# Mix and experts in one block, full units first, keys split step by step, half of the residual loaded early

## What is computed

```python
# x: [8, 1024, 256]
x = x + attn_ref(layernorm(x), ...)       # time mix (a scan over the tokens) and channel mix
x = x + ffn_ref(layernorm(x), ...)        # mixture of experts

def ffn_ref(x, expert_sel, keys, values): # 32 experts, 4 per token
    xt = x.reshape(-1, 256)
    gates = sigmoid(xt @ expert_sel.T)                      # [8192, 32]
    sel_val, sel_idx = top_k(gates, 4)
    gate_full = zeros.at[rows, sel_idx].set(sel_val)
    scores = relu(einsum('nd,edf->nef', xt, keys)) * gate_full   # keys   [32, 256, 128]
    return einsum('nef,efv->nv', scores, values)                 # values [32, 128, 256]
```

## Time and profile before

| | |
|---|---|
| runs | 1553.26, 1555.19, 1561.76 us; median 1555.19 |
| profiled execution | 1552.88 us, of which the span from first to last instruction is 1551.0 |
| PE busy | 1230.0 us (79%) |
| DVE busy | 1021.2 us (66%) |
| ACT busy | 782.7 us (50%) |
| POOL busy | 822.8 us (53%) |
| DMA traffic | 192.81 MB, mean 124 GB/s |

### The profile page before, as it was taken

How to read it: one execution, slowest core, us unless ns; L and a number is a source line. 1 busy time by engine, 2 the same in 40 slices (tenths; PEclk the granted TensorE clock), 3 DMA queues, 4 the chain that set the end, 5 groups by cost and what they waited for, 6 DMA issues and landing times. The chain is left out here.

```text
span 1551.0 us, 30666 instructions
## 1 busy us (share of the span) xinstructions
PE 1230.0 (79%) x8007; PEld 1118.6 (72%) x8008; DVE 1021.2 (66%) x2346; ACT 782.7 (50%) x1489; POOL 822.8 (53%) x902
## 2 busy tenths in 40 slices
PE   6799999999999999999974098988888888984000
PEld 5688888888888888888864087888888878883000
DVE  4788897878987788877746444444444444441799
ACT  3666676566764567555646045554555555542000
POOL 1524676666765676665656535555555555554000
PEclk9799999999999999999986579888889898787555
DMA  6000221212211121211163644444444444445998
GB/s 193 14 28 8 76 76 62 76 42 75 75 61 61 48 82 65 68 68 46 70 236 116 183 134 146 136 140 147 137 142 145 141 142 136 147 142 157 398 412 341
DMA packets 119841, 192.81 MB, mean 124 GB/s; under 512 B 17379, under 2 KB 93421, under 8 KB 118385
## 3 DMA queue, kind: packets, MB, share of 16 engines
q1 hardware_dynamic: 82672, 114.03, 23.2%
q0 software_dynamic: 26112, 67.68, 12.2%
q10 hardware_dynamic: 11008, 10.52, 2.0%
HBM read 101.09 MB, written 95.26 MB: 127 GB/s over the span
## 5 line engine op out<-in xcount | busy, mean ns | idle before, releaser
L1451 POOL DMA_INDIRECT expert_rows<-y,dest x288 | 285.7, 992 | 257.7 <-issue 216.1
L1180 POOL DMA_INDIRECT lists<-rows,slot x256 | 294.9, 1152 | 74.7 <-issue 71.3
L1356 PE MATMUL ps<-xt_hi,keys 128*128 128x128 f32 x1152 | 261.5, 311 | 56.0 <-ACT keys L1400 41.6
L1356 PEld LDWEIGHTS ps<-xt_hi,keys 128*128 128x128 f32 x1152 | 220.1, 224 | 67.3 <-issue 63.6
L1427 DVE TENSOR_TENSOR xt_lo<-ps,xt_hi 128x512 fp32r<-128x512 f32 x144 | 99.5, 691 | 218.7 <-ACT xt_hi L1384 183.0
L1396 ACT ACTIVATE y<-ps 128x512 f32<-128x512 f32 x144 | 86.8, 603 | 183.1 <-PE ps L1372 118.5
L1356 PE MATMUL ps<-xt_lo,keys 128*128 128x128 f32 x576 | 176.6, 307 | 2.0 <-issue 2.0
L582 PE MATMUL ps<-wv_hi,k_hi 128*128 128x256 f32 x512 | 151.5, 296 | 6.7 <-issue 6.5
L584 PE MATMUL ps<-wv_lo,k_hi 128*128 128x256 f32 x512 | 148.9, 291 | 4.0 <-issue 4.0
L586 PE MATMUL ps<-wv_hi,k_lo 128*128 128x256 f32 x512 | 148.5, 290 | 2.8 <-issue 2.8
L1342 PE MATMUL ps<-consts,xr 128*128 128x128 f32 x576 | 104.6, 313 | 35.7 <-DMA xr<-lists 34.1
(11 more groups left out here) (202 smaller groups left out, 3509.8 us busy)
## 6 DMA issues: line engine op xcount, KB each, us to landing
xr<-lists SPq DMA_DIRECT2D x288, 130.0 KB
ye<-expert_rows SPq DMA_DIRECT2D x32, 1024.0 KB, 20.9
x_sb<-in_x SPq DMA_DIRECT2D x16, 512.0 KB, 3.9
residual<-xp SPq DMA_DIRECT2D x16, 512.0 KB
experts_raw<-in_expert_in SPq DMA_DIRECT2D x8, 1024.0 KB, 24.4
resid<-residual SPq DMA_DIRECT2D x4, 2048.0 KB, 16.2
out_dram<-resid ACTq DMA_DIRECT2D x32, 256.0 KB, 8.3
expert_rows<-y,dest POOLq DMA_INDIRECT x288
```

Source lines behind the costliest of these rows:

```text
L1180: pool.indirect_dma_start(lists, bass.IndirectOffsetOnAxis(ap=slot[:, q, n:n + 1], axis=0), rows[:, q, n // TOPK, :], None).then_inc(held_ ...
L1356: mm = pe.matmul(ps[:, H + q % HBANKS, c], keys[:, q, s, half, k * DE:(k + 1) * DE], m[:, q, k, c], start=n == 0, stop=n == 3 * KD - 1)
L1451: pool.indirect_dma_start(expert_rows, bass.IndirectOffsetOnAxis(ap=dest[:, r, s:s + 1], axis=0), y[:, r, s, :], None, bounds_check=OUT_RO ...
```

## The change

- The blocks of the mix and of the experts become one: both functions return a routine for each engine, and an engine goes from its mix routine to its expert routine without a barrier. What the barrier ordered is ordered by waits: SyncE waits for the plan and for all scatters but the last tile's; the compute engines for the plan and for the split weights. Two tiles that the last scatters read (`rows_odd`, `slot`) get places of their own.
- The plan has two parts for each expert. First come the units that are full before the last tile's rows are counted (whole units of the count then), for all 32 experts; then the rest. The tables for this have 64 rows instead of 32. SyncE's steps up to EARLY (104 of 144) read full units only; behind that it waits for the last scatters, the fills and the cleared area.
- The keys are no longer split beforehand: `experts_raw` keeps them. Only the values are split, all eight pieces ahead of the last tile's routing. In each step ScalarE rounds the keys of both units (two instructions of 128x256), and VectorE makes their lo parts one step later (two subtractions of 128x256), the first thing in its step. TensorE waits for these.
- The residual's first two pieces are loaded by SyncE before the fills, as soon as the last tile's channel mix is done with the memory they take; the other two after the last product.
- The wait of SyncE for the last store of `residual` moves ahead of the fills; SyncE and ScalarE no longer wait behind their fills.

```diff
+EARLY = ((N - TILE) * TOPK - E * (UNIT - 1)) // UNIT // (SUB * RING) * RING
-ROUND_FIRST, SPLIT_FIRST = 3, 4
-HELD = 8
+ROUND_FIRST = 6
+RESID_AHEAD = 2
@@ program
         with ExitStack() as mix:
-            mix_phase(nc, mix, sem, locals())
+            mixing = mix_phase(nc, mix, sem, locals())
...
+            running = expert_phase(nc, experts, sem, locals())
+            with nc.Block() as block:
+                @block.sync
+                def _(sp):
+                    mixing[0](sp)
+                    running[0](sp)
...
@@ mix_phase, SyncE
             run(sp, step)
-            fill(sp, 0, E // 2)
             for stored in x1_stored:
                 sp.wait_ge(stored, 16 * NT // 2)
+        sp.wait_ge(val_ready, NT)
+        for n in range(RESID_AHEAD):
+            load_resid(sp, resid, residual, resid_loaded[0], n)
+        fill(sp, 0, E // 2)
@@ fill
-        eng.wait_ge(filled, 16 * E)
@@ round_experts, ScalarE
-                act.activation(experts_w[:, 0, part(n), :], experts_raw[:, part(n), :],
+                act.activation(values_hi[:, part(n), :], experts_raw[:, part(n), KD * DE:],
                                ACT.Copy).then_inc(experts_rounded, 1)
@@ mix_phase, VectorE
-                    split_experts(0, SPLIT_FIRST)
+                split_experts(0, LOADS)
...
             make_plan()
-            dve.wait_ge(scattered[1], 16 * (NT // 2 * J * TOPK - HELD))
-            split_experts(SPLIT_FIRST, LOADS)
@@ overflow_homes
+            chained_over(dve.tensor_copy(blocks_i[:], count[:]))
+            chained_over(dve.tensor_scalar(blocks_i[:], blocks_i[:], UNIT.bit_length() - 1, None,
+                                           ALU.logical_shift_right))
+            chained_over(dve.tensor_copy(early[:], blocks_i[:]))
+            dve.tensor_copy(units[:, 0:E], early[:])
+            dve.tensor_copy(offset[:, 0:E], early[:])
+            dve.tensor_copy(full_late[:, 0:E], zeros[:, 0:E])
+            chained_over(dve.tensor_copy(full_late[:, E:PARTS], full[:]))
@@ mix_phase, GpSimd
             run(pool, step)
-            pool.wait_ge(scattered[0], 16 * NT // 2 * J * TOPK)
-            pool.wait_ge(scattered[1], 16 * (NT // 2 * J * TOPK - HELD))
-            pool.wait_ge(held_scattered, 16 * HELD)
@@ expert_phase, SyncE
-            loop(sp, step)
+        sp.wait_ge(plan_ready, 1)
+        sp.wait_ge(scattered[0], 16 * NT // 2 * J * TOPK)
+        sp.wait_ge(scattered[1], 16 * (NT // 2 - 1) * J * TOPK)
+        for i in range(RING):
+            step(i, i, 0)
+        with sp.Fori(1, EARLY // RING) as ring:
+            for r in range(RING):
+                step(RING * ring + r, r, ring)
+
+        sp.wait_ge(last_scattered, 16 * J * TOPK)
+        sp.wait_ge(filled, 16 * E)
+        sp.wait_ge(area_cleared, 16 * (LIST_ROWS - OVERFLOW) // UNIT)
+        with sp.Fori(EARLY // RING, NSTEPS // RING) as ring:
+            for r in range(RING):
+                step(RING * ring + r, r, ring)
         sp.wait_ge(y_done, NSTEPS)
-            for n in range(RESID_PIECES):
+        for n in range(RESID_AHEAD, RESID_PIECES):
+            load_resid(sp, resid, residual, resid_loaded[1], n)
@@ expert_phase, ScalarE
-                    act.activation(keys[:, q, 1], w[:, :, bass.ds(e, 1), 0:KD * DE].rearrange(
-                        "p h a w -> p (h a) w"), ACT.Copy).then_inc(keys1_ready, 1)
+                for s, e in enumerate(experts):
+                    ins = act.activation(keys[:, q, s, 0, :], raw_keys(e), ACT.Copy)
+                ins.then_inc(keyhi_ready, 1)
@@ expert_phase, VectorE
+            if lagging(i, K_LAG):
+                b, q = i - K_LAG, (r - K_LAG) % SLOTS
+                if r == 0:
+                    expert[b % RING if isinstance(b, int) else RING - 1] = of_units(dve, plan_expert, b, E - 1)
+                dve.wait_ge(keyhi_ready, b + 1)
+                for s, e in enumerate(expert[(r - K_LAG) % RING]):
+                    ins = dve.tensor_tensor(keys[:, q, s, 1, :], raw_keys(e), keys[:, q, s, 0, :].bitcast(F32),
+                                            ALU.subtract)
+                ins.then_inc(keylo_ready, 1)
             if enters(i):
-                    dve.tensor_copy(keys[:, q, 0], w[:, :, bass.ds(expert[r], 1), 0:KD * DE].rearrange(
-                        "p h a w -> p (h a) w").bitcast(F32)).then_inc(keys0_ready, 1)
```

1840 lines of the change are left out of this document (931 added, 909 removed).

## The result

The changed kernel took 1580.91, 1577.33, 1573.04 and 1585.0 us, median 1579.12, beside 1554.54 for the kernel before on the same chip. The ratio of the runs is 1.0143, 95% interval 1.0104 to 1.0182 (the two medians alone would give 1.0158). Forecast were 1544, range 1532 to 1560. The profiled execution of after has a span of 1579.1 us, that of before 1551.0.

What follows compares the result with a forecast made beforehand. GpSimd's burst of four scatters was taken to pace the expert loop. 1552.9 − 7.5 (middle) − 8.5 (end) + 6 (loop) = 1542.9, raised to 1544 because the profiled execution lay under the median; range 1532 to 1560.

Steps and rivals of the forecast that it cites:

- that the mix stands still: Mix, ahead of everything the change touches: the prediction gave it no term.
- I take GpSimd's burst as the pace-setter.: Expert loop: GpSimd's four scatters per two-step period set its length; each 0.1 us a period is 7.2 us in all.
- The 0.08 us a period, +6 in all: Expert loop: VectorE's subtractions lengthen GpSimd's issues by 0.08 us a period, +6 us; bounds 0 and +18.
- slower: TensorE's slack ends: Expert loop rival: VectorE's holds reach the next y, 20 us each, giving 1558; decides from 16 us; chance 0.17.
- over 2: Expert loop, sign of the held case: TensorE waits for lo keys or `xt_lo` over 2 us a period.
- The second half, 8.9 us, lay beside the fills and is gone: nothing by itself.: Middle, beside the fills: dropping VectorE's second half of the split, 8.9 us, changes the time by nothing.
- Barrier and wait: Middle: without the barrier and the wait for fills the first load comes earlier, gain 6.9 to 8.4, taken as -7.5 us.
- The end: After the last product: less residual to load and possibly a shorter DRAIN, gain 6.2 to 10.7, taken as -8.5 us.
- Loads ahead, ScalarE, the plan.: Two residual loads before the fills, ScalarE's extra instruction a step, seven plan instructions: each taken as 0.

Runs made afterwards that it cites:

- the pause: One small GpSimd instruction and a wait for it, some 0.5 us, ahead of the 15th scatter of each tile; in the kernel before 1554.7 us against 1579.4.
- l1: Changed kernel with each of a step's two subtractions replaced by a one-operand reduction (lo part left wrong): 1593.5 us, ratio 1.0100 to the kernel before.
- b1: Kernel before, unedited, run again on a chip without stops beside the changed kernel: 1378.9 us.
- a1: Changed kernel, unedited, run again on a chip without stops: 1367.6 us, ratio 0.9915 to the kernel before.
- m2: Changed kernel with the pause, first set: 1561.3 us, ratio 0.9889 to the kernel before.
- m4: Changed kernel with the pause, the same kernel as m2 on another chip: 1563.6 us, ratio 0.9896 to the kernel before.
- m1: Kernel before with `rows_odd` and `slot` placed outside the mix's own tiles, no instruction added or moved: 1584.7 us, ratio 1.0064 to the unedited one.
- m3: Kernel before with the pause: 1554.7 us, ratio 0.9850 to the unedited one.
- f1: Changed kernel with GpSimd waiting for the 32 fills before the last tile's 16 scatters: 1597.4 us, ratio 1.0103 to the kernel before.

## Why the prediction was wrong

- **The step that failed most: that the mix stands still.** The prediction has no term for it, since no instruction of it moves. It took 23.0 of the 28.1 us. The kernel before holds the same 20 us as a lottery of its own (1554 on one chip, 1560 to 1581 and 1568 to 1590 on the next two, 1555 there with the pause). Its three runs, 8.5 us apart, were a sign, and so were the two tiles of 52.9 and 57.1 us in its trace, a weaker one, as they are longer than the rest without stops too. I read neither. My range took in only the terms that I had added up.
- **"I take GpSimd's burst as the pace-setter."** Wrong as it stands. Taking the lengthening away from GpSimd (l1) didn't shorten the loop, and without stops TensorE sets the pace. The 0.08 us a period, +6 in all, was the right effect but too small (mean issue 992 to 1043 ns is 14.7 us in all, 0.20 a period, within the 0 to 18), and on an engine that doesn't count: where stops are, the loop grew by 14.2 to 18.2 us, and where they aren't, it shrank by 4.9, with the mean issue at 995 ns in b1 and 994 in a1. The rival "slower: TensorE's slack ends" named the side; its price of 20 us for one hold was near the 18.2, and the loop with the pause passes the 16 us at which it was to decide. Its mechanism isn't shown, however: TensorE waits for the lo keys 0.5 us a period and not over 2, and I didn't separate it from what ScalarE does more (0.83 us a step for its two roundings, where the copy took 0.63). The copies of 0.42 us became two subtractions of 0.42 each, not of 0.30 (below), which is a term mis-sized on the way.
- **"The second half, 8.9 us, lay beside the fills and is gone: nothing by itself."** Wrong with stops. It had held GpSimd's scatters back (2.47 us), and in the trace SyncE goes on with its fills then: the eight that were left are issued from 871.24 to 876.82, while four scatters are held back (868.31 to 877.4). In after SyncE issues its 8th fill at 890.37 and nothing for 8.4 us, until the last scatter (896.85) is over. The fills took 25.1 to 26.4 us in after and its edits m2, m4 and l1, 19.9 to 21.0 in before, m1 and m3, and 13.9 with GpSimd silent (f1). I had seen the one half of this, and not that a slower engine can be a help to others. No run puts the second half back alone, so that it is this and nothing else of the change is my reading of the traces. Without stops the fills are alike in both, 16.8 and 16.7.
- **Barrier and wait.** Right: -7.5 forecast, -8.7 in the handoff without stops, and -8.9 with them before the fills' +4.1 is added. The load was not held behind the fills; it took 2.8 us to TensorE's first work.
- **The end.** Right in sign and mis-sized: -8.5 forecast, -4.8, -6.4 and -1.7 measured, of which -4.8 and -1.7 lie below my lower bound of 6.2. GpSimd's DRAIN stayed as long as before, and the loads of `ye` waited for it. The first went out 19.4 us behind the first residual load, where the lower bound had 18.2:

```profile
L135 POOLq DRAIN  x1: 7257/7257/7257, 1461.4 to 1461.4; - x1
```

  Without stops the scatters trail the last product by more (the last ends 10.4 us behind the first residual load in a1, 6.9 in after), so that the wait for them and the DRAIN, and not the residual, is most of the stretch: `ye` is issued at 22.8 of 27.9 us.
- **Loads ahead, ScalarE, the plan.** Nothing for the loads and 0.5 us for the plan (`fill_row` behind the last store), as forecast. For ScalarE nothing is shown without stops only; with them it is among what could have lengthened the loop.

On the chip without stops the sum comes close (forecast -10.0 in the profiled execution, measured -11.0), but that is luck: the terms were 0 for the mix, -7.5 for the handoff, +6 for the loop and -8.5 for the end, and measured were +4.3, -8.7, -4.9 and -1.7. Only the handoff is right there for its reason. The loop's error and those of the mix and the end cancel.

What stays open: what the stops are. They come with GpSimd's issues in close order (its scatters stood in all stretches where I saw them, and with GpSimd silent the fills ran freely), they show in SyncE's queue, in ScalarE's fills at the same instants, and in TensorE's short products, and they are there in the first result and in the first two sets, and nearly gone in the three later ones, each on another chip, with the same program. So chip and time go together here. Whether they are the chip's, the host's, the hour's or come with the recording of the trace, no run here tells. And open is which of the loop's edits costs the 14 to 18 us where they are.
